# Local attention in a two-pass macaron block: where the probabilities are turned, how the values product is split over row groups, and the order of VectorE and GpSimd

## What is computed

```python
def attn_layer(x, ...):          # 16 heads of 64, window 32
    q, k, v = split(x @ Wqkv)
    q, k = l2norm(q) * qs, l2norm(k) * ksc
    q = q * cos * scale + rotate_half(q) * sin * scale
    k = k * cos / scale + rotate_half(k) * sin / scale
    # each window of 32 queries sees its own 32 keys and the 32 before them
    sim = einsum('bhwie,bhwje->bhwij', q_w, k_look) * 8.0
    attn = softmax(where(mask, -max, sim), -1)
    return einsum('bhwij,bhwje->bhwie', attn, v_look) @ Wo
def ffn_layer(x, ...):
    a, gate = split(layernorm(x) @ W1 + b1)
    return (a * gelu(gate)) @ W2 + b2
for i in range(6):
    x = attn_layer(shift_tokens(x), ...) + x
    x = ffn_layer(shift_tokens(x), ...) + x
```

## Time and profile before

| what | value |
| --- | --- |
| time, median of 3 runs | 4861.91 us (4856.91 to 4863.68) |
| profiled execution, its own time | 4867.3 us |
| its span, first to last instruction | 4865.3 us |
| TensorE busy, of the span | 4442.0 us, 91% |
| VectorE | 2874.9 us, 59% |
| GpSimd | 2755.8 us, 57% |
| ScalarE | 2272.1 us, 47% |
| matmul of the turned probabilities (L288) | 1536 instructions, 204.3 us |
| matmuls of `gather` (L297) | 1536 + 1536 instructions, 217.6 + 219.2 us |
| mean granted TensorE clock | 0.917 |

### The profile page before, as it was taken

One profiled execution on the slowest core, in us unless ns is written; L12 is line 12 of the kernel. 1 busy time (PEld: TensorE's weight loads), 2 busy tenths in 40 slices (PEclk: granted clock), 3 DMA queues, 4 the chain that ended last, 5 costly groups with the idle time before them and its releaser, 6 DMA issues. The chain is left out here.

```text
span 4865.3 us, 144953 instructions
## 1 busy us (share of the span) xinstructions
PE 4442.0 (91%) x63640; PEld 2974.4 (61%) x63640; DVE 2874.9 (59%) x3808; ACT 2272.1 (47%) x2592; POOL 2755.8 (57%) x3515
## 2 busy tenths in 40 slices
PE   7799879999999999999866777799999999999997
PEld 3333336776766776776545665467776776777674
DVE  1366147777767777777432222577677677777773
ACT  2254225555555555555410000355555555555553
POOL 0000058777777777777322210677777777777772
PEclk9799989999999999999865555899999999999998
DMA  0000010000000000000000000100000000000000
GB/s 14 5 1 1 4 53 10 11 7 19 2 16 10 15 11 7 2 2 2 1 8 4 5 4 3 53 11 11 15 11 2 16 11 15 11 7 2 2 2 9
DMA packets 14465, 47.84 MB, mean 10 GB/s; under 512 B 3712, under 2 KB 6272, under 8 KB 12032
## 3 DMA queue, kind: packets, MB, share of 16 engines
q1 hardware_dynamic: 13824, 38.42, 2.3%
HBM read 37.37 MB, written 1.05 MB: 8 GB/s over the span
## 5 line engine op out<-in xcount | busy, mean ns | idle before, releaser
L718 POOL TENSOR_TENSOR w_qk<-w_turned 128x1024 f32<-128x1024 f32 x384 | 904.2, 2355 | 116.0 <-DVE w_turned L601 85.8
L596 DVE TENSOR_TENSOR w_turned<-w_ps_qk,w_rot_l 128x1024 f32<-128x1024 f32 x384 | 469.7, 1223 | 713.9 <-ACT w_squares L498 694.6
L255 PE MATMUL w_ps_qk<-w_w_qk,ZT 128*128 128x512 f32 x1536 | 751.2, 612 | 37.5 <-DVE w_turned L601 17.6
L305 PE MATMUL w_ps_y<-w_px,w_w_vo 128*128 128x128 f32 x6144 | 751.2, 276 | 6.9 <-ACT w_px L502 6.7
L305 PEld LDWEIGHTS w_ps_y<-w_px,w_w_vo 128*128 128x128 f32 x6144 | 721.0, 192 | 31.8 <-issue 21.1
L747 POOL TENSOR_TENSOR w_qk<-w_qk,w_inv_norm 128x1024 f32<-128x1024 f32 x384 | 722.9, 1904 | 0.0
L498 ACT ACTIVATE w_squares<-w_ps_qk 128x1024 f32<-128x1024 f32 x384 | 391.2, 1019 | 437.0 <-PE w_ps_qk L255 436.5
L601 DVE TENSOR_TENSOR w_turned<-w_ps_qk,w_rot_l 128x1024 f32<-128x1024 f32 x384 | 466.1, 1214 | 0.0
L605 DVE TENSOR_REDUCE w_sumsq<-w_squares 128x16 f32<-128x1024 f32 x384 | 455.2, 1185 | 0.0
L502 ACT ACTIVATE w_px<-w_ps_t 128x1024 f32<-128x1024 f32 x192 | 196.5, 1024 | 507.0 <-PE w_ps_t L297 507.0
L879 POOL MEMSET n_sel<- 128x512 f32 x6 | 3.2, 527 | 754.9 <-POOLq L1014 362.5
(11 more groups left out here) (256 smaller groups left out, 7545.9 us busy)
## 6 DMA issues: line engine op xcount, KB each, us to landing
w_w_qk<-in_w_qk SPq DMA_DIRECT2D x12, 1024.0 KB, 4.8
w_w_vT<-in_w_vT SPq DMA_DIRECT2D x12, 512.0 KB, 3.7
w_w_o<-in_w_o SPq DMA_DIRECT2D x12, 512.0 KB, 5.1
w_w<-in_w SPq DMA_DIRECT2D x12, 384.0 KB, 3.1
w_w<-in_w SPq DMA_DIRECT2D x12, 192.0 KB, 3.1
XT<-in_x SPq DMA_DIRECT2D x1, 1024.0 KB, 4.5
w_rot<-in_rot SPq DMA_DIRECT2D x2, 512.0 KB, 5.7
out<-XT SPq DMA_DIRECT2D x1, 1024.0 KB, 3.9
```

The costliest lines, as they stand in the source:

```text
L255: last = nc.tensor.matmul(ps_qk[:, c, :], Z[:, T.col:T.col + P], w_qk[:, T.parity, cols], start=True, stop=True)
L305: last = nc.tensor.matmul(ps_y[:, D.t * P:(D.t + 1) * P].rearrange("p (a v q) -> p a v q", a=2, q=WIN), w_vo[:, D.parity, h, p, :], px[:, ...
L596: nc.vector.tensor_tensor(turned[:, which, 0, :].rearrange("p (h d) -> p h d", d=DH), flat(ps_qk[:]).rearrange("p (h d) -> p h d", d=DH), ...
L718: nc.gpsimd.tensor_tensor(qk[:, T.odd, which, :], turned[:, which, 0, :], turned[:, which, 1, :], ALU.add).then_inc(pool_add, 1)
```

## The change

Seven things change in `windowed_layers`, and nothing outside it.

1. `turn_probs` and ScalarE's copy of its result are gone. VectorE transposes `probs` into `pT` itself, with one instruction on 128 partitions x 1024 elements that transposes each 32x32 block by itself. The partition then is a key within its window of 32, the blocks of the four windows stand on four groups of 32 partitions, and `pT` is [P, 2 halves, 16 heads, 32 queries].
2. `gather` becomes one piece of eight matmuls. Each contracts 32 keys (32 partitions, one row group of four) and has 512 columns: all 16 heads of one window. Half 0 (the keys before the window) and half 1 (its own) accumulate in the same bank, one bank for each window, four in all: `ps_w`, of which `ps_t` and `ps_s` are now the halves.
3. `windows` becomes `tokens`: two transpositions a tile in place of four, no extra ones at a sequence's start. ScalarE copies 256 columns in place of 512.
4. On TensorE the whole `gather` of tile C now stands between the key projection and `scores(B)`. `scores` waits until ScalarE has copied the upper two banks of `ps_w` (`act_px`), which it overwrites.
5. On VectorE the row sums and the reciprocal of tile C stand first in the step, ahead of `rotate(T, 0)`. The transposition follows `rotate(T, 0)` (and `down`'s addition). The maximum and the subtraction of tile B move from the middle to the end of the step, behind the second `sum_squares` and the chain of small instructions.
6. On GpSimd the multiplication of the probabilities stands ahead of `add(T, 0)`.
7. The pieces of the feed-forward sit in other places: `place_1` ahead of the key projection, `bc` and the variance (`cen`) between `gather` and `scores`.

The core of the diff:

```diff
-            def turn_probs(C):
-                for p in range(PAIRS):
-                    last = nc.tensor.transpose(ps_t[:, p // 4, (p % 4) * P:(p % 4 + 1) * P],
...
-            def gather(C, half, bank):
-                for v in range(2):
-                    w = 2 * half + v
-                    for h in range(2):
-                        rows = slice(h * KEYS, (h + 1) * KEYS)
...
+            def gather(C):
+                for half in range(2):
+                    for w in range(WINS):
+                        rows = slice(w * WIN, (w + 1) * WIN)
+                        last = nc.tensor.matmul(ps_w[:, w, :], x_tok[rows, C.t, half, :],
+                                                pT[rows, half].rearrange("p h q -> p (h q)"),
+                                                start=half == 0, stop=half == 1)
                 last.then_inc(pe_px, 1)
...
+                place_1(s)
                 if T:
                     pe.wait_ge(dve_turn, T.n * 2 + 1)
                     project(T, 1, pe_k)
-                place_1(s)
                 if C:
                     if B:
                         pe.wait_ge(act_tk, B.n + 1)
-                    pe.wait_ge(pool_p, C.n + 1)
-                    turn_probs(C)
+                    pe.wait_ge(dve_sub, C.n + 1)
+                    pe.wait_ge(dve_pt, C.n + 1)
+                    pe.wait_ge(act_xt, C.n + 1)
+                    gather(C)
                 place_2(s)
                 if B:
                     pe.wait_ge(act_tk, B.n + 1)
-                    if D:
-                        pe.wait_ge(act_px, D.n * 2 + 2)
-                    elif C:
-                        pe.wait_ge(dve_sub, C.n + 1)
+                    if C:
+                        pe.wait_ge(act_px, C.n * 2 + 1)
                     scores(B)
...
+                if C:
+                    dve.wait_ge(pool_p, C.n + 1)
+                    if D:
+                        dve.wait_ge(pe_px, D.n + 1)
+                    nc.vector.transpose(pT[:].rearrange("p a h q -> p h a q"),
+                                        probs[:].rearrange("p h (a k) -> p h a k", a=2)).then_inc(dve_pt, 1)
```

More of the change, by code:

```diff
@@ L263, in turn, with tokens @@
                 last.then_inc(done, 1)
[L265 to L268, removed]
+            def tokens(B):
+                for half in range(2):
+                    at = B.col - WIN * (1 - half)
+                    last = nc.tensor.transpose(ps_f[:, half * P:(half + 1) * P], Z[:, at:at + P], ident[:])
+                last.then_inc(pe_xt, 1)
             def scores(B):
@@ L389, in place_3 @@
                     last.then_inc(pe_var, 1)
-                if s.bc:
-                    if s.merge():
-                        layer, parity, quarters = s.merge()
-                        pe.wait_ge(act_m, layer * 4 + quarters[1] + 1)
-                    elif s.bias():
-                        layer, parity = s.bias()
-                        pe.wait_ge(dve_bias, layer + 1)
-                    pe.wait_ge(dve_var, s.bc.m + 1)
-                    pe.wait_ge(pool_rstd, s.bc.m + 1)
-                    for t in range(TILES):
-                        last = nc.tensor.matmul(ps_f[:, t * P:(t + 1) * P], rstd[:, t:t + 1].broadcast_to([P, P]),
-                                                ident[:], start=True, stop=True, skip_group_check=True)
-                    last.then_inc(pe_bc, 1)
+                if s.gate:
+                    gate(s.gate, 1)
+                if s.up:
+                    up(s.up, 1)
+            def place_3(s):
+                if s.B and s.k % TILES == 0:
+                    if s.cen:
+                        pe.wait_ge(dve_var, s.cen.m + 1)
+                    tokens(s.B)
+                if s.bc and s.merge():
+                    layer, parity, quarters = s.merge()
+                    pe.wait_ge(act_m, layer * 4 + quarters[1] + 1)
+                    broadcast(s)
                 if s.gate:
@@ L406, in place_3, with broadcast @@
                     up(s.up, 2)
-            def place_4(s):
-                if s.B and s.k % TILES == 0:
-                    if s.cen:
-                        pe.wait_ge(dve_var, s.cen.m + 1)
-                    tokens(s)
-                if s.edge:
-                    if s.gate:
-                        pe.wait_ge(act_gate, s.gate.m * FFB + FFB)
-                    elif s.k == 2:
-                        pe.wait_ge(dve_bias, L0 + 1)
-                    else:
-                        pe.wait_ge(act_xt, s.B.n + 1)
-                    windows(s.edge, s.edge.col - 3 * WIN, 2, pe_xe)
+            def broadcast(s):
+                if s.bias():
+                    layer, parity = s.bias()
+                    pe.wait_ge(dve_bias, layer + 1)
+                pe.wait_ge(dve_var, s.bc.m + 1)
+                pe.wait_ge(pool_rstd, s.bc.m + 1)
+                for t in range(TILES):
+                    last = nc.tensor.matmul(ps_f[:, t * P:(t + 1) * P], rstd[:, t:t + 1].broadcast_to([P, P]),
+                                            ident[:], start=True, stop=True, skip_group_check=True)
+                last.then_inc(pe_bc, 1)
             def gate(f, i):
@@ L628, in step @@
                 if T:
[L629 removed]
+                    if T.k % PER == 0:
+                        dve.wait_ge(pool_rot, T.layer + 1)
+                    rotate(T, 0)
                 if s.down:
@@ L758, in step @@
                                             ALU.mult).then_inc(pool_p, 1)
+                if T:
+                    add(T, B, 0, pe_tq)
                 if A:
```

155 lines of the change are left out of this document (64 added, 91 removed).

## The result

The changed kernel takes **4921.2 us** (median; 4918.2 to 4929.0), against 4862.1 for the kernel before: ratio 1.0126, 95% interval 1.0108 to 1.0143. It is **1.3% slower**; forecast was 4760, 2.1% faster, with a range of 4680 to 4880. The profiled execution took 4922.7 us.

The account below looks back on a forecast made before the run. It took TensorE, 98.5% busy, as the bound before, and a ring of waits after: profiled 4867.3 - 94 (ring) - 20 (merges) + 12 (GpSimd's table scaling) = 4765, runs' median 5 lower: 4760 us. Range 4680 to 4880.

Parts of the forecast that it names:

- D: How late VectorE's maximum starts after the scores end on TensorE: 0.1 to 0.2 us, 0.8 in up, 0.3 in down steps.
- sum of squares and chain 1.95: VectorE's sum of squares of the keys and small instructions after it, ahead of the maximum: 1.95 us.
- 7.2 against 7.1: From the key projection's start: 7.2 us until VectorE is ready for the maximum, 7.1 for product, copy and scores.
- every miss counts in full: No-change rival: the ring has no slack; 0.5 us more per pass removes 96 us; chance 0.10 for within 0.2%.
- The ring: Chain of waits from one tile's scores to the next's, setting step times: four steps 67.55 us against 69.5, saving 94.
- a merge: Merge of a quarter, in two bc steps of four, moves into the keys' turn wait: 1.1 us saved, 20 times.
- The product: TensorE's values product as two rounds of four matmuls on four row groups: 1.9 us, before 2.12.
- the page's 3.07: The Trainium skill's speedup for four row tiles of K=32, N=512; would make the product 2.24 us, 65 us more in all.
- the keys' turn: TensorE's turning of the keys, waiting for ScalarE's qT: some 1.1 us idle ahead of it in bc and gate steps.
- the masks: TensorE's mask matmuls ahead of the scores, waiting for ScalarE's copy of the upper banks: 0.2 to 0.45 us everywhere.
- VectorE or GpSimd becomes the bound in up steps: Rival: VectorE has some 16.9 us of work in up steps; at 18, 4840 to 4890 us; chance 0.07 for slower.
- would fit into 16: GpSimd, busy 75%, 13 us of a 17.6 us step, would also fit into a step of 16 us.

Follow-up runs that it names:

- number 1: The changed kernel with a padded layout for the 36 sums of squares and two helpers, used by VectorE's four small chain instructions: 4799.5 us, ratio 0.9851.
- padded_after_twice: The changed kernel with do-nothing TensorE instructions added, placed as in padded_twice: 4902.2 us, ratio 1.0083.
- padded_twice: square_some with do-nothing TensorE instructions added to shift the program's place modulo 256, in their second placement: 4723.1 us, ratio 0.9717.
- square_some: number 1 with ScalarE squaring the queries ahead of the exponential in bc and gate steps only: 4769.8 us, ratio 0.9805.
- number 2: The changed kernel with GpSimd executing its addition of the turned keys twice: 5472.8 us, ratio 1.1260.
- chain_last: The changed kernel with VectorE's chain of four small instructions moved behind the subtraction: 4841.7 us, ratio 0.9951.

## Why the prediction was wrong, step by step

- **The step that failed is D**, the sum with the term "sum of squares and chain 1.95", which gave 7.2 against 7.1. The 1.95 was read where the chain stood before, behind the subtraction, with GpSimd mostly at something else. At its new place it meets the keys' addition each time. D was forecast at 0.1 to 0.8, 0.35 on average, and is 1.05 on average (1.20 in nearly every step). By the prediction's own "every miss counts in full" that is 0.70 x 192 = 134 us, and number 1 measured 122 (134 by the ratios).
- **The second miss is a cost that stood in no row I used**: the supply of instructions inside the scores. It was 4 gaps in the trace of before, 14.2 us with the short ones, and is 30 gaps and 52.9 us after it. With the collision they cost some 19 us (padded_after_twice against the changed kernel), without it 47 (padded_twice against square_some).
- **The ring held in sum, in part by luck.** With D near the forecast's (0.16, 0.09, 0.09 and 0.75 in number 1's down, bc, gate and up steps) the median steps of the four kinds add up to 17.82 + 16.75 + 16.31 + 16.97 = 67.85 us; forecast was 18.75 + 15.8 + 16.5 + 16.5 = 67.55. But most bc steps hold a merge or a bias, which the forecast reckoned apart: a bc step with neither takes 15.44 us. So four plain steps are 66.5 us, 1.0 less than forecast, most of it in the down step; before they were 69.8 (forecast 69.5). And a bc step with a merge was 1.8 us longer than a plain one before and still is 1.3 longer in number 1: a merge saves 0.5 us, where 1.1 was forecast. The errors partly cancel. Number 1 came to 4799.5, not 4760; the 47 us of the gaps are as large as this difference.
- **The operations held.** The product is 1.93 us (forecast 1.9): its 16 records start at 1529.53, the next group at 1531.46 (rows below). So the row was the right one, and the estimate from the page's 3.07, 2.24 us, is too long here (the page names no type for its figure; "another type" was my addition). The transposition is 1.24 us (forecast 1.2), and no probabilities are waited for ahead of the product.
- **The waits held in place, not in size**: the keys' turn waits 156.0 us for ScalarE's qT in the changed kernel and 58.2 in number 1, where about 1.1 in half of the steps, some 105, was forecast; the masks 38.4 us, 0.2 a step, the low end of 0.2 to 0.45. Unforeseen is the wait of the tokens' transposition for `xn` (43.5 us, 14.3 in number 1), as VectorE is late.
- **The rivals.** "VectorE or GpSimd becomes the bound in up steps" was the nearest in time (4840 to 4890) with the wrong mechanism. It was not VectorE's sum of work that slowed it but one small instruction that stood still. That GpSimd "would fit into 16" counted its busy time only, not what it shuts out.
- **The clock** is 0.98 in the stretch of the earlier trace rows, where 1.00 was asked for; the output product's matmuls keep their 276 ns, so it costs next to nothing here. In number 2 the same matmuls take 305 ns.

```profile
1529.53 2.00 PE L287 MATMUL w_ps_w<-w_pT,w_x_tok 32*128 32x512 f32 x16
1531.46 1.05 PE L374 MATMUL w_ps_f<-mean_col,w_xn_sq 128*128 128x1 f32 x8
```

## What to carry to other kernels

When VectorE's work is moved, look at what GpSimd does at the new place, not only at how long it is busy: a tiny SBUF-to-SBUF tensor_scalar can stand still for a whole GpSimd instruction, and if it lies in a ring of waits, that counts in every step. A layout that keeps it out of the two-port mode cost nothing here (ratio 1.0002). When a dense group of small matmuls comes behind a new wait, read the "issue" gaps inside the group; if they always fall at the same instruction, it is the program's position that decides, and a few added instructions move it.

## What the runs showed of the hardware

- A VectorE tensor_scalar of 128x36 float32, SBUF to SBUF, lasts 182 ns alone, and 660 to 1328 ns beside GpSimd's 2.36 us addition in the changed kernel, ending 0.04 us after it. One that starts with the addition, as in number 2, lasts up to 2.3 us. With the padded layout it is 191 ns, beside GpSimd or not.
- TensorE's instructions come in transfers of 16 KB, that is 256 instructions. If one starts only inside a group of 256 instructions in 1.5 us, and the place falls in the last third of the group, TensorE stands still: 1.3 to 3.0 us in the changed kernel, up to 3.3 in chain_last, until 1.2 to 1.7 us after it landed. The Trainium skill (Runtime: NRT & Kernel Launch, "Instruction fetch mechanics") gives the same blocks and calls the cost of crossing into the next one "mostly hidden"; in the changed kernel's scores 30 of 70 crossings were not. What sets off the transfer was not settled.
- An added wait that has long been met lasts 51 ns in the records. 99 and 213 of them ahead of a stack cost 6.6 and 18.7 us. padded_twice has 464 and 599 of them in the program of the two stacks' steps and is still 47 us faster.
- VectorE transposes 128x1024 float32 in blocks of 32 in 1.24 us.
